# Self loops of a graph convolution counted once in attention instead of added by identity matmuls in each layer

## The reference

```python
def _gcn_conv(x, src, dst, W, b, n_nodes):
    h = x @ W
    loops = jnp.arange(n_nodes, dtype=src.dtype)
    s = jnp.concatenate([src, loops])
    d = jnp.concatenate([dst, loops])
    deg = jax.ops.segment_sum(jnp.ones_like(d, dtype=h.dtype), d, num_segments=n_nodes)
    dis = jnp.where(deg > 0, jax.lax.rsqrt(deg), 0.0)
    norm = dis[s] * dis[d]
    out = jax.ops.segment_sum(h[s] * norm[:, None], d, num_segments=n_nodes)
    return out + b

h = jax.nn.relu(_batch_norm(_gcn_conv(x, src, dst, W1, b1, n), g1, be1))
h = jax.nn.relu(_batch_norm(_gcn_conv(h, src, dst, W2, b2, n), g2, be2))
h = jax.nn.relu(_gcn_conv(h, src, dst, W3, b3, n))
h = _gcn_conv(h, src, dst, W3, b3, n)
```

## Time and profile before

| what | us |
|---|---|
| median of three runs (4518.91 to 4523.36) | 4519.57 |
| the profiled execution | 4507.92 |
| its span, from the first to the last instruction | 4506.1 |
| busy in it: PE / DVE / ACT / POOL | 3795.1 / 2229.2 / 1808.0 / 1668.2 |
| attention, first to last gather issue | 194.7 to 2324.3 |
| convolutions, first matmul to the end of the span | 2756.5 to 4506.1 |

### The profile page before, as it was taken

The page is one execution under the profiler, slowest core; times in us unless marked ns, Lnnn a source line. Parts: engine busy times, 40 slices in busy tenths (PEclk is TensorE's granted clock), DMA queues, the critical chain, the costliest instruction groups (busy, mean ns, idle before and its releaser), DMA issues. The chain is left out here.

```text
span 4506.1 us, 70127 instructions
## 1 busy us (share of the span) xinstructions
PE 3795.1 (84%) x22077; PEld 2348.0 (52%) x22077; DVE 2229.2 (49%) x3464; ACT 1808.0 (40%) x4859; POOL 1668.2 (37%) x1597
## 2 busy tenths in 40 slices
PE   2598888888888888888766767999899989999998
PEld 2365565555555565555544545444544454444444
DVE  6687788778788788887764443000200020002001
ACT  2277777777777777777742224000200020002000
POOL 0377777777777777777740000000000000000000
PEclk7678777777778778787866667999999999999999
DMA  5233333333333333333330002665456545654664
GB/s 167 86 104 95 97 94 95 94 97 94 94 94 98 95 99 96 97 94 95 97 91 21 10 4 79 198 201 193 145 196 203 178 159 195 204 173 165 199 200 138
DMA packets 470145, 556.02 MB, mean 123 GB/s; under 512 B 38090, under 2 KB 417106, under 8 KB 469934
## 3 DMA queue, kind: packets, MB, share of 16 engines
q1 hardware_dynamic: 390702, 369.08, 25.5%
q0 software_dynamic: 51168, 107.68, 10.6%
q10 hardware_dynamic: 28224, 78.69, 4.6%
HBM read 453.72 MB, written 103.18 MB: 124 GB/s over the span
## 5 line engine op out<-in xcount | busy, mean ns | idle before, releaser
L783 POOL DMA_INDIRECT fts<-ft_tab,src_all x1568 | 1652.0, 1054 | 477.7 <-issue 477.7
L1990 PE MATMUL cv_acc<-cv_cnt,cv_parts 128*128 128x512 bf16 (+1 forms) x7644 | 1566.0, 367 | 0.0
L1990 PEld LDWEIGHTS cv_acc<-cv_cnt,cv_parts 128*128 128x128 bf16 x7644 | 722.2, 98 | 822.6 <-issue 2.2
L1843 DVE TENSOR_TENSOR cv_y<-cv_acc,cv_dis_row 128x512 f32<-128x512 f32 (+1 forms) x52 | 34.3, 660 | 1448.3 <-PE cv_acc L1997 1448.3
L814 DVE TENSOR_TENSOR ohk<-iota_ps,key_cols 128x784 bf16<-128x784 f32 x784 | 720.7, 955 | 0.0
L1063 PE MATMUL agg_ps<-terms,oh 128*64 128x141 f32 x2744 | 614.9, 406 | 29.7 <-DVE terms L849 28.0
L1953 ACT ACTIVATE cv_sd<-cv_mv,eps 128x1 f32<-128x1 f32 x4 | 1.2, 294 | 1579.3 <-DVE cv_tmp L1895 1579.3
L904 ACT ACTIVATE dist_l<-lo_iota,low 128x128 bf16<-128x128 f16 x1960 | 593.7, 387 | 7.0
L1063 PEld LDWEIGHTS agg_ps<-terms,oh 128*64 128x64 f32 x2744 | 532.4, 205 | 77.9 <-DVE terms L849 64.5
L1024 PE MATMUL ftd_ps<-win,ohdT 64*128 64x130 f32 x3136 | 326.2, 332 | 271.7 <-DVE prod L828 271.4
L1002 PE MATMUL adj_ps<-ohk,ohl 128*128 128x196 bf16 x3136 | 423.3, 261 | 62.1 <-ACT strip L952 43.7
(11 more groups left out here) (255 smaller groups left out, 2921.5 us busy)
## 6 DMA issues: line engine op xcount, KB each, us to landing
cv_cnt<-adj SPq DMA_DIRECT2D x96, 2048.0 KB, 8.0
cv_cnt<-adj SPq DMA_DIRECT2D x48, 2176.0 KB, 8.3
adj<-strip ACTq DMA_DIRECT2D x196, 392.0 KB
fts<-ft_tab,src_all POOLq DMA_INDIRECT x1568
win<-ft_tab SPq DMA_DIRECT2D x196, 65.0 KB
agg_tab<-res SPq DMA_DIRECT2D x196, 35.2 KB
cv_cnt<-adj SPq DMA_DIRECT2D x8, 512.0 KB, 3.7
agg_tab<-zero_f SPq DMA_DIRECT2D x5, 705.0 KB
```

Source lines behind the costliest of these rows:

```text
L783: nc.gpsimd.indirect_dma_start(fts[u][:, k, :], None, ft_tab[:, :], bass.IndirectOffsetOnAxis(src_all[:, n, k:k + 1], 0)).then_inc(gathere ...
L1990: last = nc.tensor.matmul(a[:, 0:width], parts[:, r, b, :], cnt[q][:, 0:width // SUB, (b - b0) * SUB:(b - b0 + 1) * SUB], start=(b == 0 an ...
```

## The change

The self loops become part of the counts in `adj`. A constant `own` has ones where a source equals its destination: seen through a window that `k.j` moves, 392 columns of a 32-row matrix give the ones of one quarter, and `own_low`, shifted by `k.u`, puts them into the right 32 of the 128 rows. In `count(k, q)` one matmul with these two opens the quarter's PSUM bank (`start=True`), and the four count matmuls add to it. DVE makes both constants at the start of attention (two memsets and two copies), and PE waits for them once. In `convolutions` the identity matmuls and the semaphore `acc` are gone; DVE waits for the last chunk's `cnt_used` instead. A count can now be one higher, so the test for counts that bf16 can't hold compares with 255.

```diff
--- before.py
+++ after.py
@@ -639,8 +639,9 @@
 
 def attention(nc, t, sb, pb, sem, g):
 
-    ft_tab, row_tab, agg_tab, adj, sched, src_all, shared, ident, spots, key_cols, low_cols = (g[k] for k in (
-        "ft_tab", "row_tab", "agg_tab", "adj", "sched", "src_all", "shared", "ident", "spots", "key_cols", "low_cols"))
+    ft_tab, row_tab, agg_tab, adj, sched, src_all, shared, ident, ident_bf, spots, key_cols, low_cols = (g[k] for k in (
+        "ft_tab", "row_tab", "agg_tab", "adj", "sched", "src_all", "shared", "ident", "ident_bf", "spots", "key_cols",
+        "low_cols"))
     LD = 6
     QS = 2
     QC = QS * SC
@@ -663,6 +664,8 @@
         terms = sb("terms", [P, 2, GC, WA], F32, c)
         res = sb("res", [WD, UN, WA], F32, c)
         iota_sb = sb("iota_sb", [P, KEYS + P], F32, c)
+        own = sb("own", [SUB, NA, 2 * KEYS], BF16, c)
+        own_low = sb("own_low", [SUB, 2 * P - SUB], BF16, c)
         lo_iota = sb("lo_iota", [P, P], FP16, c)
         ohk = sb("ohk", [P, 2, NA * SC, KEYS], BF16, c)
         ohl = sb("ohl", [P, 2, NA * SC, P], BF16, c)
@@ -676,6 +679,7 @@
         most_ps = pb("most_ps", [P, 512], F32, c)
         iotas = sem("iotas")
         consts = sem("consts")
+        own_made = sem("own_made")
         win_in = [sem(f"win_in{u}") for u in range(UN)]
         rows_in = [sem(f"rows_in{h}") for h in range(2)]
         gathered = [sem(f"gathered{u}") for u in range(UN)]
@@ -791,6 +795,12 @@
             nc.vector.memset(signs[:, 1:2], RS).then_inc(consts, 1)
             nc.vector.memset(rows[:], 1.0).then_inc(consts, 1)
             nc.vector.memset(fade[:], 1.0).then_inc(consts, 1)
+            nc.vector.memset(own[:], 0.0).then_inc(own_made, 1)
+            nc.vector.memset(own_low[:], 0.0).then_inc(own_made, 1)
+            dve.wait_ge(own_made, 2)
+            nc.vector.tensor_copy(own[:, :, KEYS:KEYS + HALF], ident_bf[0:SUB, 0:SUB].rearrange("p (a d) -> p a d", d=HALF)
+                                  ).then_inc(own_made, 1)
+            nc.vector.tensor_copy(own_low[:, P - SUB:P], ident_bf[0:SUB, 0:SUB]).then_inc(own_made, 1)
             for s in range(2):
                 nc.vector.memset(terms[:, s, :, WA - 1:WA], 1.0).then_inc(consts, 1)
             dve.wait_ge(iotas, 1)
@@ -996,11 +1006,17 @@
                     pe.wait_ge(ohl_done, k.n + 1)
                 if q >= 2 or k.after(1):
                     pe.wait_ge(strip_done, 4 * k.n + q - 1)
+                settle(pe, tick_pe)
+                if isinstance(k.j, int):
+                    tile_of = own[:, q * QS:(q + 1) * QS, KEYS - HALF * k.j:2 * KEYS - HALF * k.j]
+                else:
+                    tile_of = own[:, q * QS:(q + 1) * QS, ds(KEYS - HALF * k.j, KEYS)]
+                nc.tensor.matmul(adj_ps[q % 2][:, 0:QS * KEYS], own_low[:, P - SUB - SUB * k.u:2 * P - SUB - SUB * k.u], tile_of, start=True, stop=False)
                 for a in range(QS):
                     for m in range(SC):
                         n = q * QC + a * SC + m
                         last = nc.tensor.matmul(adj_ps[q % 2][:, a * KEYS:(a + 1) * KEYS], ohl[:, k.s, n, :],
-                                                ohk[:, k.s, n, :], start=(m == 0), stop=(m == SC - 1))
+                                                ohk[:, k.s, n, :], start=False, stop=(a == QS - 1 and m == SC - 1))
                 last.then_inc(adj_done, 1)
 
             def nearness(k):
@@ -1104,6 +1120,7 @@
                 if k.exists():
                     first_features(k)
             zero = Group(0, 0, 0)
+            pe.wait_ge(own_made, 4)
             nearness(zero)
             closeness(zero)
             steps(pe, body, 2)
@@ -1145,7 +1162,7 @@
                                         z[:, b, :].unsqueeze(3).to_broadcast([P, BATCH, H, DH]), ALU.mult)
             low = odd[:, 0:NT * H].rearrange("p (t h) -> p t h", h=H)
             link(nc.vector.tensor_scalar(low, raw[:, :, HD:HD + H], FAINT, None, ALU.is_lt))
-            nc.vector.tensor_scalar(odd[:, NT * H:NT * H + NT], deg[:], 256.0, None, ALU.is_gt).then_inc(deg_made, 1)
+            nc.vector.tensor_scalar(odd[:, NT * H:NT * H + NT], deg[:], 255.0, None, ALU.is_gt).then_inc(deg_made, 1)
             dve.wait_ge(deg_made, 1)
             link(nc.vector.tensor_tensor(low, low, deg[:].unsqueeze(2).to_broadcast([P, NT, H]), ALU.mult))
             nc.vector.tensor_reduce(odd_n[:], odd[:], AX.X, ALU.add).then_inc(odd_made, 1)
@@ -1713,7 +1730,7 @@
         tile_no = sb("cv_tile_no", [P, NT], F32, c)
         w_ps = [pb(f"cv_w_ps{u}", [P, 2, 512], F32, c) for u in range(2)]
         acc = [pb(f"cv_acc{s}", [D, GRP], F32, c) for s in range(2)]
-        names = ("par_in", "const", "row_ps", "row", "staged", "w_ps", "hs", "first_part", "split", "acc",
+        names = ("par_in", "const", "row_ps", "row", "staged", "w_ps", "hs", "first_part", "split",
                  "y", "vch", "dch", "var", "sd", "ready", "out_ps", "sum", "tick", "tick_pe", "tick_sp",
                  "tick_pool", "iotas", "table_out", "idx_in", "rows_in", "chunk_over", "oh", "part_ps",
                  "gch", "fch", "loop_free")
@@ -1839,7 +1856,7 @@
                 settle(dve, s["tick"])
 
                 def finish_group(n, u, use, at, width, real, stat):
-                    dve.wait_ge(s["acc"], n + 1)
+                    dve.wait_ge(cnt_used[2], n + 2)
                     nc.vector.tensor_tensor(y[:, 0:width], acc[u][:, 0:width], dis_row[:, at], ALU.mult
                                             ).then_inc(acc_read[u], 1)
                     dve.wait_ge(acc_read[u], use + 2)
@@ -1989,14 +2006,8 @@
                         for r in range(3):
                             last = nc.tensor.matmul(a[:, 0:width], parts[:, r, b, :],
                                                     cnt[q][:, 0:width // SUB, (b - b0) * SUB:(b - b0 + 1) * SUB],
-                                                    start=(b == 0 and r == 0), stop=False)
+                                                    start=(b == 0 and r == 0), stop=(b == NT - 1 and r == 2))
                     last.then_inc(cnt_used[q], 1)
-                for b in range(width // P):
-                    for r in range(3):
-                        w = parts[:, r, ds(tile0 + b, 1), :].rearrange("p a d -> p (a d)")
-                        last = nc.tensor.matmul(a[:, b * P:(b + 1) * P], w, ident_bf[:], start=False,
-                                                stop=(b == width // P - 1 and r == 2))
-                last.then_inc(s["acc"], 1)
 
             pe.sem_inc(s["hs"], 2)
             with pe.Fori(0, L) as l:
```

## The result

The changed kernel took 4466.09 us in the median of five runs (4461.74 to 4479.63); the kernel before, run beside it, 4521.06 us (4518.91 to 4523.61). The ratio is 0.988, with a 95% interval of 0.9864 to 0.9895: faster by 55 us, or 1.2%. Forecast were 4487 us and a gain of 32.8 us. The profiled execution took 4461.7 us, 46.2 us less than that of the kernel before. (Both kernels were timed again later in other sets of runs.

A forecast was written before the change was run, and what follows sets the result against it. PE bounds the convolutions, POOL's gathers bound attention. Layers -32.8 us, attention 0 and startup 0 take 4519.6 us to 4486.8, say 4487; the forecast's own range is 4479 to 4495, the 8-in-10 range 4454 to 4506.

The forecast's parts named there:

- rival 2: Attention's gathers: more PE work throws DVE out of step, fewer gathers collide with its weighting; 17 to 43 us gained; chance 0.15.
- Removed, -32.8 us: Convolutions: 588 identity matmuls at 55.6 ns each go from a PE-bound chain, saving 32.8 us.
- Counts' transfers hidden, startup 0: Strip counts land in 24.3 us within a 31.73 us period; making the constants takes some 3.3 us; both cost 0.
- Added, 1.06 us per round, into a cover of 1.77: Attention: four new matmuls with increments and addresses cost PE 1.06 us per group, inside its 1.77 us wait for DVE's product.
- the high end of 1.72: Attention: the added work per group at half clock, 4 x (0.33 + 0.10) = 1.72 us, said to just fit the cover.
- Attention: 0: Attention's length stays POOL's 2129.7 us of gathers, 10.87 us per group, so the added PE work costs 0.
- Rival 1: Attention slows as half-clock PE rounds reach 13.8 us; +27 us at a third of rounds, +163 at half; chance 0.15.
- If the cover were gone, 1.06 us x 196 = 208 us would be bare: Attention: the added PE work's whole price, 208 us over 196 groups, if PE's wait no longer hid it.

The follow-up runs named there:

- two PSUM kernels: Kernel before and changed kernel, each with DVE copying the exponentials into PSUM so the weighting has one SBUF operand: 4339.33 and 4306.13 us.
- layers-only runs: Kernel before without identity matmuls, old attention kept, self loops left out of the result: 5363.3 us against 5393.8, and 5281.7 against 5316.9.
- startup-only kernel: Kernel before plus the two constants made by DVE and PE's wait for them, never used: 5393.2 us against 5393.8.
- ordinary executions: Runs in which the unchanged kernel before took 4521.06 us (first comparison) or 4513.7 us (second set of runs).
- sets 1 and 3: Sets of runs where the unchanged kernel before took 5393.8 and 5316.9 us; the changed kernel took 5660.4 and 5567.4 us.

## Why the prediction was right, and where it wasn't

The time fell inside the range of 4454 to 4506 us, and faster had 0.88. But it fell outside the forecast's own range of 4479 to 4495, in the part that was there for rival 2: the direction and the layers' term were right by their mechanism, the rest of the gain came by a mechanism that I had priced and not chosen.

- **Removed, -32.8 us: right.** 33.5 us in the profile, 33.2 us as the difference of the two PSUM kernels, 30.5 and 35.2 us in the layers-only runs. The pitch of 55.6 ns and not the mean of 219 ns was the right price.
- **Counts' transfers hidden, startup 0: right.** `own` was cleared in 1.36 us, not 2.7: it is written as 1568 words of 32 bits, a form that my row of 16-bit elements did not show. The startup-only kernel differs by 0.6 us, though it ran only where POOL is not the bound.
- **Added, 1.06 us per round, into a cover of 1.77: right in kind.** PE's idle time before the features fell by 127.6 us and that before the counts by 62.1 us, less 16 us before the new matmul: 174 us, 0.89 us per round. The 1.77 us were one round's; the mean wait before the features was 271.7 / 196 = 1.39 us, so the high end of 1.72 would not have fitted in every round. In the ordinary executions none of it reached the path.
- **"Attention: 0": the step that failed.** It was -19.3 us. The forecast held POOL's 2129.7 us for fixed because POOL waits for nothing. But an engine that never waits can still be slowed by a neighbour, and 172 us of its time were that; the added work moved DVE against it. This is rival 2, priced at 17 us for a tenth of the groups. 25 fewer of the gathers were over 1.5 us (154 instead of 179). It had 0.15 and deserved more, since the rows showed one long gather per group, always at the weighting, and DVE tied to the landings. Of the 21 us between 4487 and 4466, it takes 19.
- **Rival 1: refuted where I looked for it.** In the ordinary executions of the changed kernel POOL never waits for `terms_done`. In sets 1 and 3 its sign and its sign of being wrong, POOL waiting for `terms_done`, came true, but not by its mechanism: it hung on PE's rounds at half clock, and there DVE's chain behind a late `most` sets the round. The clock is lower too (0.75 over the span against 0.84); what share it has was not told apart. "If the cover were gone, 1.06 us x 196 = 208 us would be bare" named the danger, and its size against the measured 294 is partly luck.
- The median of before lies some 13 us above its profiled execution, that of after 4 us. I took the first as the run's own; nothing tells where it lies. It is why the medians differ by 55 us and the profiled executions by 46.

## What to carry to other kernels

A cover is a property of one execution's order of arrivals, not of the code: before work is put into a wait, ask what is left if the wait moves to another instruction, and price the work bare. In sets 1 and 3 even that price was too low, it seems because 0.7 us more made another instruction late. The bound engine's busy time deserves the same look as its idle time: where the mean of an instruction (1054 ns) is above its median (944 ns), find what runs beside the long ones, and remove that first; here a 0.23 us copy bought 174 us, three times the change's own 55. And time a change in more than one set of runs before trusting its sign. Work removed from an unbroken chain is worth its start-to-start time, to a few per cent.

## What the runs showed of the hardware

- A DVE multiplication with both inputs in SBUF holds up a gather that POOL issues during it: the gather ends 0.8 us after the multiplication does (1.89 us for 0.94). With one input in PSUM it doesn't (no gather of the 1568 over 0.97 us).
- Added matmuls can raise the granted clock and so pay for a part of themselves: it was 0.78, 0.80 and 0.86 with none, one and two more per quarter, and the first cost 149 us of PE's busy time in 1850 us, the second 19.
- The same kernel took 4514 to 4521 us in some sets of runs and 5317 to 5394 in others. The stretch of the layers kept its length there (1716 us without the identity matmuls), attention's round took 15.3 us instead of 10.9, and PE, DVE and ACT stood idle for 4 to 7 us of most rounds while POOL issued gathers, though the transfers' packets ended as soon as always; a change can have the opposite sign there.
